# The ball block of a three-part transformer kernel: two staged blocks joined into one step-by-step schedule

## The reference, cut to what matters

```
ada = t_emb @ w_ada + b_ada                       # six modulation rows per batch
xm  = expmap0(layer_norm(logmap0(x)) * (1 + sc_msa) + sh_msa)
q, k, v = plin(xm, w_q, b_q), ...                 # plin(x,w,b) = expmap0(logmap0(x) @ w + b); 256 -> 256 each
q, k, v = per head (16 heads of 16), each limited to the ball
attn = softmax(q k^T / sqrt(16)) @ v              # 512 x 512 per head
attn_t = g_msa * logmap0(plin(from_heads(attn), w_o, b_o))
x   = mobius_add(x, expmap0(attn_t))              # x2, y2, xy per row; a tanh per row
xm  = expmap0(layer_norm(logmap0(x)) * (1 + sc_mlp) + sh_mlp)     # a logarithm per row
ff  = plin(plin(xm, w_f1, b_f1), w_f2, b_f2)      # 256 -> 1024 -> 256, a norm over the 1024
out = mobius_add(x, expmap0(g_mlp * logmap0(ff)))
```

## Time and profile before

| | us |
|---|---|
| median of 3 runs | 3969.59 (3960.39 to 3975.46) |
| the profiled execution itself | 3953.57 |
| its span, first to last instruction | 3951.8 |

### The profile page before, as it was taken

One profiled execution on the slowest core, in us unless ns is written; L12 is line 12 of the kernel. 1 busy time (PEld: TensorE's weight loads), 2 busy tenths in 40 slices (PEclk: granted clock), 3 DMA queues, 4 the chain that ended last, 5 costly groups with the idle time before them and its releaser, 6 DMA issues. The chain is left out here.

```text
span 3951.8 us, 51774 instructions
## 1 busy us (share of the span) xinstructions
PE 3543.2 (90%) x18664; PEld 2033.0 (51%) x18664; DVE 2053.1 (52%) x5521; ACT 1616.6 (41%) x3088; POOL 557.1 (14%) x160
## 2 busy tenths in 40 slices
PE   8999999999954888889649994899999999999998
PEld 3555555555541343434336672455555555555564
DVE  3334333433445344444354434877777777777773
ACT  2333333333321444445312221555555555555552
POOL 0000000000006434343110001111111111111110
PEclk9999999999987889999768886999999999999999
DMA  4011001011010000000000004000000000000000
GB/s 155 30 57 56 31 33 57 30 36 51 9 65 32 7 5 5 5 3 2 28 3 12 8 5 154 19 19 22 19 20 22 19 20 27 29 28 25 19 23 27
DMA packets 77535, 120.30 MB, mean 30 GB/s; under 512 B 10313, under 2 KB 66532, under 8 KB 72050
## 3 DMA queue, kind: packets, MB, share of 16 engines
q1 hardware_dynamic: 77298, 117.20, 8.6%
HBM read 96.16 MB, written 16.83 MB: 29 GB/s over the span
## 5 line engine op out<-in xcount | busy, mean ns | idle before, releaser
L2370 PE MATMUL wps<-w_wqkv,w_hT 128*128 128x512 f32 x768 | 377.3, 615 | 3.1 <-DMA w_wo<-in_wwo 3.1
L2408 PE MATMUL wps<-w_xnT,w_w 128*128 128x512 f32 (+1 forms) x768 | 351.5, 598 | 24.5 <-DVE w_xnT L2233 20.3
L1992 POOL TENSOR_TENSOR w_rn<-w_n,w_mhalf 128x16 f32<-128x16 f32 x64 | 187.5, 2930 | 1095.2 <-DVE w_n L2170 1095.2
L1179 POOL TENSOR_TENSOR bb_routh<-bb_rinh,b_expo 128x51 f32<-128x51 f32 x32 | 271.7, 8496 | 187.4 <-DVE bb_rinh L1279 187.4
L2020 ACT ACTIVATE w_pr<-w_sm,w_nmx,w_rn 128x256 f32<-128x256 f32 (+1 forms) x512 | 286.5, 562 | 10.0 <-DVE w_nmx L2151 9.4
L603 PE MATMUL ps<-xT,rw 128*128 128x512 f32 x512 | 245.6, 602 | 0.2 <-DMA rb<-in_eb 0.2
L2408 PEld LDWEIGHTS wps<-w_xnT,w_w 128*128 128x128 f32 (+1 forms) x768 | 133.2, 178 | 217.3 <-issue 193.7
L1391 PE MATMUL bb_ps<-bb_qT,bb_kT 32*128 32x512 f32 x1024 | 188.4, 689 | 62.9 <-ACT bb_pr L1189 51.6
L619 PE MATMUL ps<-hid,rw 128*128 128x512 f32 x512 | 240.7, 592 | 0.0
L2370 PEld LDWEIGHTS wps<-w_wqkv,w_hT 128*128 128x128 f32 x768 | 137.4, 192 | 131.7 <-issue 126.6
L2007 ACT ACTIVATE w_pT<-wps 128x512 f32<-128x512 f32 (+1 forms) x128 | 69.6, 544 | 329.1 <-PE wps L2317 329.1
(11 more groups left out here) (307 smaller groups left out, 6560.2 us busy)
## 6 DMA issues: line engine op xcount, KB each, us to landing
rw<-in_ew SPq DMA_DIRECT2D x32, 1024.0 KB, 6.7
w_xa<-xs SPq DMA_DIRECT2D x16, 512.0 KB, 3.9
w_xin<-xs SPq DMA_DIRECT2D x64, 128.0 KB, 3.8
xT<-in_xT SPq DMA_DIRECT2D x8, 512.0 KB, 4.1
xres<-in_x SPq DMA_DIRECT2D x32, 128.0 KB, 2.2
x<-x1t SPq DMA_DIRECT2D x32, 128.0 KB, 1.7
b_x<-x SPq DMA_DIRECT2D x1, 4096.0 KB, 14.1
xs<-b_w SPq DMA_DIRECT2D x8, 512.0 KB, 3.0
```

Source lines behind the costliest of these rows:

```text
L1179: g.tensor_tensor(routh[:, q % 2], rinh[:, q % 2], expo[:, 1, 0:HW], ALU.pow).then_inc(root_ok, 1)
L1992: g.tensor_tensor(rn[:, i % 2, t], n2[:, n % 2, 1], mhalf[:], ALU.pow).then_inc(nr_ok, 1)
L2370: ins = te.matmul(to, hT[:, i % 2, k, t * P:(t + 1) * P], wqkv[:, i // B, k, s * 512:(s + 1) * 512], start=(k == 0), stop=(k == KD - 1))
L2408: ins = te.matmul(to[0:n], w1[:, i // B, k, lo:lo + n], xnT[:, k], start=(k == 0), stop=(k == KD - 1))
```

## The change

The second and the third block become one unrolled block. A batch now passes through steps that are counted from its first attention step: its rows are made at -27 to -24, its four tiles are projected from -21 on, `w_o` comes at 18 and 19, the vector additions and norms from 21 to 34 (now for the 4 tiles of one batch, columns of shape 128x4), the turn at 35, `w_f1` at 37 to 42, the hidden norm at 45, `w_f2` at 45 to 49, the second addition and the output from 51 to 59. A batch begins every 16 steps, so in the middle three batches are under way. `STEPS` has 199 steps instead of 169; in the last 44 there is no attention.

The hidden squares are now summed over the 8 slices by POOL (one copy and seven additions of 128x512), and the norm needs 4 one-column matmuls per batch instead of 32. All side jobs on PE (all but scores and values) share a ring of three PSUM banks, 5 to 7: `claim` waits until the job three places earlier in the ring has been read out. Values use bank 4 alone. `y`, `u`, `raw`, `rcp`, `rinh` and `routh` are there once. The two exponentials of a step follow one wait; the queries are copied out of PSUM by ACT, the keys by DVE. `w` for all tiles is gone. The product and the sum of `x` and `w` are one DVE instruction (`tensor_tensor_reduce`). `spread` uses a transpose. The weights of the feed-forward part are loaded at the start of the joined block, ahead of the first modulation rows on SP.

```diff
-            LEAD = 25
-            STEPS = range(-LEAD - 8, S * B + 8)
+            LEAD = 21
+            STEPS = range(-LEAD - 6, S * (B - 1) + 60)
+            F1 = {37: (0,), 38: (1,), 39: (2, 3), 41: (4, 5), 42: (6, 7)}
+            F2 = {45: 0, 46: 1, 47: 2, 49: 3}
+            YS = {46: 0, 47: 1, 48: 2, 50: 3}
...
+            for G in STEPS:
+                for job in side_jobs(G):
+                    place[job] = (5 + len(place) % 3, len(place) // 3)
...
             def _(sp):
+                for dst, name in ((wf1, "wf1"), (bf1, "bf1"), (wf2, "wf2"), (bf2, "bf2")):
+                    sp.dma_start(dst[:], io[name]).then_inc(ld_f, 16)
...
+                def squares_summed(b, m):
+                    n = b * MF + m
+                    pool.wait_ge(f_a, n + 1)
+                    if m == 0:
+                        if b:
+                            filled(pool, "fn", b - 1)
+                        g.tensor_copy(acc[:], fsq[:, 0]).then_inc(acc_ok, 1)
+                    else:
+                        pool.wait_ge(acc_ok, n)
+                        g.tensor_tensor(acc[:], acc[:], fsq[:, m % 2], ALU.add).then_inc(acc_ok, 1)
+
+                for G in STEPS:
+                    for asked in roots_asked(G):
+                        root(*asked)
+                    if among(G, F1):
+                        for m in among(G, F1)[1]:
+                            squares_summed(among(G, F1)[0], m)
...
+                def update_squares(b, t):
...
+                    if t % 2 == 0:
+                        a.activation(junk[:, (n - 1) % 2], product, ACT.Square, accum_out=YA2[:, c:c + 1]).then_inc(sq_ok, 1)
+                    else:
+                        a.activation(junk[:, 2], product, ACT.Square, accum_out=YA2[:, c:c + 1]).then_inc(done(f"wo{t // 2}", b), 1)
...
+                def projected(q):
+                    t = q % NT
+                    if q:
+                        dve.wait_ge(ysq_ok, q)
+                        dve.wait_ge(z_ok, 2 * q)
+                    filled(dve, "qk", q)
+                    v.scalar_tensor_tensor(out=y[:, 0:2 * D], in0=bank("qk", q), scalar=lim[:, 0, t:t + 1], in1=bqkv[:, 0:2 * D],
+                                           op0=ALU.mult, op1=ALU.add).then_inc(done("qk", q), 1)
...
+                for G in STEPS:
+                    if group_due(G, 0) is not None:
+                        take(group_due(G, 0))
+                    if tile_due(G, 6) is not None:
+                        limit_heads(tile_due(G, 6))
+                    if tile_due(G, 2) is not None:
+                        projected(tile_due(G, 2))
+                    if group_due(G, 1) is not None:
+                        divide(group_due(G, 1))
...
+                    if group_due(G, 0) is not None:
+                        invert(group_due(G, 0))
...
+                def claim(*job):
+                    k, n = place[job]
+                    assert place[job] == (5 + turn[0] % 3, turn[0] // 3), job
+                    turn[0] += 1
+                    if n:
+                        pe.wait_ge(free[k], n)
+                    return bank(*job), full[k]
...
+                def hidden_norms(b):
+                    pe.wait_ge(acc_ok, (b + 1) * MF)
+                    to, ready = claim("fn", b)
+                    for t in range(NT):
+                        ins = te.matmul(to[:, t:t + 1], acc[:, t * P:(t + 1) * P], ones[:, 0:1], start=True, stop=True)
...
+                for G in STEPS:
+                    if attends(G + 1):
+                        scores(G + 1)
+                    if tile_due(G, 1) is not None:
+                        heads(tile_due(G, 1), "qk", 0, 2 * D)
+                    if group_due(G, 1) is not None:
+                        spread(group_due(G, 1))
+                    if tile_due(G, 7) is not None:
+                        turn_heads(tile_due(G, 7))
+                    if tile_due(G, 0) is not None:
+                        turn_rows(tile_due(G, 0))
+                    if at(G, 35) is not None:
+                        turn_rows2(at(G, 35))
+                    if attends(G):
+                        values(G)
+                    if tile_due(G, 1) is not None:
+                        heads(tile_due(G, 1), "v", 2 * D, 3 * D)
+                    if group_due(G, 0) is not None:
+                        row_sums(group_due(G, 0))
...
```

More of the change, by code:

```diff
@@ L1112, in due, with among, tile_due @@
+            def among(G, table):
+                for after, what in table.items():
+                    if at(G, after) is not None:
+                        return at(G, after), what
+                return None
+            def tile_due(G, after):
                 q, rest = divmod(G + LEAD - after, NT)
                 return q if rest == 0 and 0 <= q < NQ else None
-            def rows_due(G):
-                f, t = divmod(G + LEAD + 8, S)
-                return (f, t) if 0 <= f < B and t < NT else None
@@ L1120, in batch_due @@
-            def batch_due(G, after):
-                f, rest = divmod(G + LEAD - after, S)
-                return f if rest == 0 and 0 <= f < B else None
             def group_due(G, after):
@@ new lines, in ball_block, with bank, filled, emptied @@
+            place = {}
+            for G in STEPS:
+                for job in side_jobs(G):
+                    place[job] = (5 + len(place) % 3, len(place) // 3)
+            def bank(*job):
+                return ps[:, place[job][0]]
+            def filled(eng, *job):
+                k, n = place[job]
+                eng.wait_ge(full[k], n + 1)
+            def emptied(eng, *job):
+                k, n = place[job]
+                eng.wait_ge(free[k], n + 1)
+            def done(*job):
+                return free[place[job][0]]
@@ L1221, in _ @@
[L1221 to L1235 removed]
+                        act.wait_ge(root_ask, rank["h", q - 1])
@@ new lines, in applied @@
+                def applied(b):
+                    for t in range(b * NT, b * NT + NT):
+                        n = ch.mark(v.tensor_scalar(x[:, t], x[:, t], FX[:, t:t + 1], None, ALU.mult))
+                    ch.wait(n)
+                    for t in range(NT):
+                        n = ch.mark(v.scalar_tensor_tensor(out=x[:, b * NT + t], in0=wa[:, t], scalar=FW[:, b * NT + t:b * NT + t + 1],
+                                                           in1=x[:, b * NT + t], op0=ALU.mult, op1=ALU.add))
+                    ch.wait(n)
@@ new lines, in row_norms @@
+                def row_norms(b):
+                    c = columns(b)
+                    r = slice(b * NT, b * NT + NT)
+                    carry_wait()
+                    for t in range(NT):
+                        n = ch.mark(v.bn_stats(st[:, t], x[:, b * NT + t]))
+                    ch.wait(n)
+                    carry_wait()
+                    for t in range(NT):
+                        n = ch.mark(v.bn_aggr(mv[:, b * NT + t], st[:, t]))
+                    ch.wait(n)
+                    s.tt(c(0), mv[:, r, 0], mv[:, r, 0], ALU.mult)
+                    s.tt(c(0), c(0), mv[:, r, 1], ALU.add)
+                    s.ts(c(11), c(0), float(D), None, ALU.mult)
+                    ask("r1", b, c(11), EPS * EPS)
@@ new lines, in result @@
+                def result(b, p):
+                    for t in (2 * p, 2 * p + 1):
+                        c = b * NT + t
+                        n = ch.mark(v.tensor_scalar(wb[:, t], wb[:, t], FW[:, c:c + 1], None, ALU.mult))
+                    ch.wait(n)
+                    for t in (2 * p, 2 * p + 1):
+                        c = b * NT + t
+                        ins = v.scalar_tensor_tensor(out=wb[:, t], in0=x[:, c], scalar=FX[:, c:c + 1], in1=wb[:, t],
+                                                     op0=ALU.mult, op1=ALU.add)
+                    ins.then_inc(out_ok, 1)
@@ L1380, in _ @@
                 te = nc.tensor
+                turn = [0]
+                def claim(*job):
+                    k, n = place[job]
+                    assert place[job] == (5 + turn[0] % 3, turn[0] // 3), job
[3 more added lines that the diff above has]
+                    return bank(*job), full[k]
                 def scores(G):
@@ new lines, in hidden @@
+                def hidden(b, m):
+                    if m == 0:
+                        emptied(pe, "fu0", b)
+                        emptied(pe, "fu1", b)
+                        if b == 0:
+                            pe.wait_ge(ld_f, 4 * 16)
+                    to, ready = claim(f"f{m}", b)
+                    for k in range(KD):
+                        ins = te.matmul(to, wf1[:, k, m * P:(m + 1) * P], uT2[:, k], start=(k == 0), stop=(k == KD - 1))
+                    ins.then_inc(ready, 1)
```

1031 lines of the change are left out of this document (541 added, 490 removed).

## The result

| kernel | median, us | of the kernel before, with 95% interval |
|---|---|---|
| before | 3965.0 (3960.4 to 3975.5, 4 runs) | 1 |
| changed | 3865.6 (3861.6 to 3867.3, 4 runs) | 0.974 (0.972 to 0.977) |

The account below looks back on a forecast made before the run. PE bounds the attention and feed-forward loop, with stretches without PE and half clock besides. Lead-in 77, attention 909 and end 105 make 1091 us for 1215.8, 125 less: 3829, plus 16 carried over, 3845 us (3755 to 3940).

Parts of the forecast that it names:

- the group of 15.8 us: PE work: four attention steps with one row tile's projection take 15.8 us at full clock; four groups 63.2 us.
- (a): PSUM ring: `spread` waits for `projected` to free its bank, 2.2 us in every group, 9 us per batch.
- (b): Late root of 51 columns holds `limit_heads`: asked in steps 7 and 11, 4.4 and 3.6 us late, 8 us per batch.
- (c): Step 3: the turn's second half waits for the bank of `wo0`, which ACT frees late, 3.4 us.
- (d): A step with little work beside it is bound by ACT's exponentials, 0.7 us once per batch.
- the two rows: Earlier trace: PE went on at full clock after a 1.43 us wait, at half after 3.21 us.
- rival 2: More waits: engines hold each other up and 2.2 us waits drop the clock, about 3950 us; chance 0.10, plus 0.04 to no change.
- so I add nothing: DVE beside POOL: no time added for shared-port holds, since a DVE copy took 0.43 us inside a root.
- 7 us for the single `y`: Lead-in: one `y` buffer makes a tile's loop serial at 13.8 us, adding 7 us.
- Rival 1: Shorter waits in the batches: roots in time and no clock loss, about 100 us less, 3745 us; chance 0.13.
- Rival 3: Slower: POOL's additions pass a batch's 134 us at 11 us each; chance 0.07 together with worse forms of rival 2.
- Rival 4: Feed-forward work only moves behind the attention instead of running beside it; given no chance.

Follow-up runs that it names:

- c1: Changed kernel with reordered queues together (`projected` and root question earlier, `spread` behind values, weights later, squares reordered), two `y` buffers: 3683.4 us, 0.928; again 3680.0 us.
- e5: Changed kernel with all of `projected` ahead of `limit_heads` in VectorE's order, two buffers for `y`, bf16 junk outputs: 3719.2 us, 0.937 of the kernel before.
- e6: Changed kernel with `spread` behind the values of its step in PE's order, no longer ahead of them: 3792.6 us, 0.955 of the kernel before.
- e4: Changed kernel with POOL copying each slice of hidden squares instead of adding it to the sum: 3833.0 us, 0.966 of the kernel before.
- x2: c1 with POOL's root of 51 columns replaced by a memset of the same tile (head norms wrong): 3662.7 us, 0.922 of the kernel before.
- x1: Changed kernel with most of the seventh batch's feed-forward matmuls left out (outputs not the reference's): 3862.6 us, 0.974 of the kernel before.
- e3: Changed kernel with the hidden norm's four one-column matmuls made eight times each, 32 per batch as before: 3951.0 us, 0.996 of the kernel before.
- c2: c1 with the bias of the hidden slices on ScalarE instead of VectorE: 3657.5 us, 0.922 of the kernel before.

## Why the prediction was right, and where it was not

**The sum.** 3845 against 3866 us: 125 us less forecast, 99 measured (95 by the length of the block in the traces). The attention, with most of the working, came out at 911.9 against 909, the lead-in at 81.2 against 77. The term that was mis-sized is the end, 128.1 against 105. That the attention came so close is in part luck. In a full batch 7 us too much PE work stand against 4.5 us too little waiting and 1 us of clock. Over the stretches, the third took 121.4 us and not 134, the seventh 126.4 and not 119, the eighth about 3 more than forecast.

**PE work of a full batch.** Forecast 101.4 us, measured 94.6 (c1's batch at clock 1.00). The error is the group of 15.8 us in the earlier trace rows, which I took as work at full clock. It is 14.2: e5's second stretch, at a clock of 1.00, has 64.22 us of PE work, less 7.4 for `w_o`, in four groups. The 15.8 us held a wait of 0.41 us and scores that took 2.04 us, as their second half waited for the second exponential, where 1.14 is usual. And `spread` as a transpose takes 0.63 us (four records) in place of 1.16 (eight). The scores before the change, and then e5's stretch:

```profile
1605.93 2.04 PE L1391 MATMUL bb_ps<-bb_qT,bb_kT 32*128 32x512 f32 x8 [0.41 <-ACT bb_pr L1189]
```
```profile
1366.00:1439.30 73.30, 64.22 (x409) 28.99 (x410) 45.04 (x152) 44.51 (x73) 38.83 (x9) 1.00 0.02 6
```

**The waits.** Forecast 21 us, measured 25.5. (a) `spread`'s wait for the ring, 2.2 us forecast, is 2.35 in steps 1 and 5. (b) In steps 9 and 13 it is 8.70 and 6.66, where 2.2 + 4.4 and 2.2 + 3.6 were forecast. Some 2 us of step 9 are the two operations that POOL's additions hold. (c) 3.4 us for the turn, measured 3.14. (d) 0.7, measured 0.90 and 0.71, beside 0.66 for `ya`. Each place was right; the size of step 9 was 2.1 us too small.

**The clock.** Forecast 12 us from three waits above 3 us, measured 13.0 from all five above 2 us. The wait of 2.35 us is the one that I had left between the two rows. It fell on the wrong side: right size, by three phases that cost less than I took and two that I had left out. This is what rival 2 named, and it came with the forecast's total only because PE work was 7 us less. The rule of the Trainium skill that the prediction named (TensorE: Matmul & The Clock Gate, Why this matters for your kernels), that idle gaps between bursts throw PE back to the half clock, agrees with e5 and e6: where the gaps went, the clock rose from 0.86 to 0.97 and 0.92.

**POOL.** An addition takes 1.29 us (56 of them, 72.0 us), 1 was taken. But the step "so I add nothing" failed. The copy inside a root in the earlier trace rows was no test for an addition, since the root holds nothing. The 98 `tensor_tensor` of 128x4 on the columns that lie wholly inside a root took 0.15 to 0.17 us, as they do with POOL idle. The addition does hold: beside it the same operation took up to 1.27 us. The Trainium skill's rule that DVE and GpSimd share a port pair and that one of them waits for the whole instruction of the other (SBUF — State Buffer, Who interferes with whom), which I had set aside by that row, agrees with the 1.24 us at 1801.15 and the 0.57 of e4; it disagrees with the 0.17 us inside the 8.51 us root. e4 prices the additions at 31 us in all, hold, later sums and what the clock did together.

**Lead-in.** 5 us for the weights ahead of the modulation was right (5.7 in c1). 7 us for the single `y` was wrong as a reason: with two buffers in e5 the first exponential came at 1298.8, in the changed kernel at 1299.2. The root is part of the loop from tile to tile, as x2 shows: without it the first exponential comes 23 us earlier. That VectorE's order is the rest is argued and not shown; `u`, `rinh` and `routh`, which are also there once, were not doubled in any run.

**End.** The chain to the last turn took 70.9 us against 56, the last feed-forward part 42.4 against 34, the last stretch 14.8 against 15. The step that failed is this one: I had summed the last batch's chain as if VectorE were free beside it, and then given 8 us for the seventh batch's work in the queues, thinking of PE's. x1 showed that PE's part of it costs nothing. What costs is VectorE, which in the full batches has 44% of its time free and in the 44.1 us of x1's comparison 10%. The last feed-forward part holds 35.1 us of PE work, half clock included, near the 34 forecast; the other 7.3 us are waits that I had put at nothing, 4.4 of them for POOL's sum (at 2304.47).

**Rivals.** Rival 1 (waits shorter) is what e5 and c1 had to be built for. Rival 3 (POOL) had an engine that does cost time, 31 us and not hundreds, and not by the path that it named: in a full batch POOL is busy 52.7 of 133.2 us. Rival 4 has nothing for it. That the stretches without PE are gone is right, but by e3 they are not what the time came from: without the cheaper norm, but with its additions, all the rest gives 0.4%.

## What to carry to other kernels

When a ring of buffers replaces fixed ones, look at which engine frees each place and what stands ahead of the freeing instruction in that engine's order: here one operation behind a late root, on an engine with 44% of its time free, cost 145 us of 3865, half clock included. Cover short PE waits too, since a wait can count again in the clock: in e6 34 us of cover gave 72. And price what a cheaper computation brings onto another engine: POOL's additions took some 31 of the 87 us that they had saved on PE. And where a pipeline drains, sum each engine's work anew: an engine that has room in the full steps can be the bound of the last ones.

## What the runs showed of the hardware

- The granted clock fell from 1.00 (2.4 GHz) to 0.5 (1.2 GHz) at the waits of 2.35 us in the changed kernel's full batches, and not at those of 1.35 in e6's. It is no matter of the wait alone. Ahead of the turn PE waited 2.74 us in c1 and in c2; in c1's batch the clock stayed at 1.00, in c2 it fell. And in two full batches of e4 PE waited 3.14 us there, and the clock fell once. Four matmuls of the turn took 1.11 us and then 0.66:

```profile
1759.82 1.11 PE L1874 MATMUL bb_ps<-b_ident,bb_fsq 128*128 128x128 f32 x4 [3.14 <-ACT bb_junk L1319]
...
1886.36 0.66 PE L1874 MATMUL bb_ps<-b_ident,bb_fsq 128*128 128x128 f32 x4 [3.14 <-ACT bb_junk L1319]
```

- POOL's instruction holds VectorE by kind, not by length: the 8.51 us power did not, the 1.29 us addition and the 0.61 us copy did. VectorE's kind counts as well. The bias of a hidden slice, which reads PSUM, took its usual 0.75 us wholly inside an addition, and so did the row statistics (0.42 us):

```profile
1813.88 1.27 POOL L1281 TENSOR_TENSOR bb_acc<-bb_acc,bb_fsq 128x512 f32<-128x512 f32 x1 [5.02 <-ACT bb_fsq L1371]
1814.10 0.75 DVE L1665 TENSOR_SCALAR bb_fT<-bb_ps,bb_bf 128x512 f32<-128x512 f32 x1 [0.97 <-PE bb_ps L1885]
```

- A memset on POOL held VectorE too. In c1 the scaling of the modulation rows ran into POOL's memset and took 1.12 us, where the changed kernel's (at 1224.97, with POOL idle) took 0.29:

```profile
1217.49 3.51 POOL L1259 MEMSET bb_val<- 128x4096 f32 x1
...
1220.02 1.12 DVE L885 TENSOR_SCALAR bb_mod<-bb_mod 128x256 f32<-128x256 f32 x1 [3.92 <-DMA bb_mod<-ada]
```
